# Attention scores as columns of the dense product, and a closed layer's bias and Relu on ScalarE

## The reference, cut to what matters

```python
def _gat_layer(x, src, dst, W, a_src, a_dst, b):
    h = (x @ W).reshape(N, H, C)
    alpha_s = jnp.einsum('nhc,hc->nh', h, a_src)
    alpha_d = jnp.einsum('nhc,hc->nh', h, a_dst)
    e = jax.nn.leaky_relu(alpha_s[src] + alpha_d[dst], NEG_SLOPE)
    m = jax.ops.segment_max(e, dst, num_segments=N)
    ex = jnp.exp(e - m[dst])
    den = jax.ops.segment_sum(ex, dst, num_segments=N)
    alpha = ex / (den[dst] + 1e-16)
    msg = h[src] * alpha[:, :, None]
    return jax.ops.segment_sum(msg, dst, num_segments=N).reshape(N, H * C) + b
for l in range(3):
    x = relu(_gat_layer(x, src, dst, W[l], att_src[l], att_dst[l], bias[l]))
```

## Time and profile before

| | us |
|---|---|
| median of three runs (12354.32 to 12355.26) | 12354.43 |
| the profiled execution's own time | 12329.05 |
| its span, first to last instruction | 12327.0 |
| POOL busy (64% of the span) | 7913.0 |
| PE busy (49%) | 6088.9 |
| DVE busy (41%) | 5089.2 |
| ACT busy (33%) | 4118.9 |

### The profile page before, as it was taken

One profiled execution on the slowest core, in us unless ns is written; L12 is line 12 of the kernel. 1 busy time (PEld: TensorE's weight loads), 2 busy tenths in 40 slices (PEclk: granted clock), 3 DMA queues, 4 the chain that ended last, 5 costly groups with the idle time before them and its releaser, 6 DMA issues.

```text
span 12327.0 us, 135596 instructions
## 1 busy us (share of the span) xinstructions
PE 6088.9 (49%) x36060; PEld 5310.7 (43%) x36060; DVE 5089.2 (41%) x15885; ACT 4118.9 (33%) x10791; POOL 7913.0 (64%) x8254
## 2 busy tenths in 40 slices
PE   0389721445555567997444434434344443444443
PEld 0288611334444446876333333433333343333333
DVE  8555300032222224223444444544444454444445
ACT  0299300034444441101333333333333323333332
POOL 2877777567777750001777777577777757777775
PEclk8555765766666667998555555555555555555555
DMA  9144521222222224886222222222222222222222
GB/s 284 37 103 103 143 59 39 55 53 53 53 53 53 53 49 134 249 255 182 67 67 67 69 67 67 59 64 69 67 68 68 67 54 69 69 67 67 69 67 59
DMA packets 1052978, 1046.24 MB, mean 85 GB/s; under 512 B 641674, under 2 KB 758198, under 8 KB 1051984
## 3 DMA queue, kind: packets, MB, share of 16 engines
q1 hardware_dynamic: 704688, 614.67, 17.2%
q0 software_dynamic: 263776, 336.86, 13.4%
q10 hardware_dynamic: 83808, 86.39, 2.1%
HBM read 938.74 MB, written 100.17 MB: 84 GB/s over the span
## 4 chain that ended last, share of the span: by engine, by line
POOL 61%; issue 21%; PE 11%; DVE 5%; DMA 1%; ACT 1%; DVEq 0%; POOLq 0%; SPq 0%; ACTq 0%; PEldq 0%
POOL sb_HG L586 48%; POOL edge_counts L639 13%; PE sums L1038 4%; PE sums L951 1%; PE psA L1038 1%; PE psB L1038 1%; PE psD L1038 1%; PE psC L1038 1%; DVE sb_HG L1322 1%; DVE sb_ACC L2050 1%; DVE sb_HG L1323 0%; PE psD L935 0%; DMA edge_counts<-sb_HG 0%; PE psB L927 0%; DMA sb_HG<-attention_table,sb_NOW 0%
## 5 line engine op out<-in xcount | busy, mean ns | idle before, releaser
L586 POOL DMA_INDIRECT sb_HG<-attention_table,sb_NOW x4980 | 4727.4, 949 | 2993.5 <-issue 1513.3
L951 PE MATMUL sums<-sb_HG 128*128 128x100 f32 x9984 | 2064.3, 398 | 443.7 <-ACT sb_HG L711 426.9
L951 PEld LDWEIGHTS sums<-sb_HG 128*128 128x128 f32 x9984 | 2031.4, 312 | 453.7 <-ACT sb_HG L711 435.9
L639 POOL DMA_INDIRECT edge_counts<-sb_HG x1625 | 1634.0, 1006 | 697.7 <-issue 490.0
L707 ACT ACTIVATE sb_H<-sb_iota_row,sb_H 128x128 f32<-128x128 f32 x6656 | 2029.2, 388 | 138.1 <-PE sums L951 65.6
L586 POOL DMA_INDIRECT sb_HG<-feature_table,sb_NOW x1612 | 1523.0, 945 | 643.2 <-issue 491.0
L2050 DVE TENSOR_TENSOR sb_ACC<-sb_ACC,sums 128x100 f32 x4992 | 1274.7, 255 | 1155.9 <-PE sums L951 618.9
L961 PEld LDWEIGHTS sums<-sb_HG 128*128 128x128 f32 x6656 | 1313.4, 297 | 328.7 <-issue 328.5
L961 PE MATMUL sums<-sb_HG 128*128 x6656 | 1329.3, 382 | 157.3 <-ACT sb_HG L711 74.5
L800 ACT ACTIVATE psC<-sb_SB 128x128 f32<-128x128 f32 x156 | 43.8, 281 | 3925.8 <-DVE sb_SB L2003 3925.8
L1570 DVE TENSOR_TENSOR sb_ACC<-sb_ACC,sums 128x97 f32 (+1 forms) x3328 | 848.2, 255 | 606.9 <-PE sums L961 127.7
(11 more groups left out here) (507 smaller groups left out, 8917.9 us busy)
## 6 DMA issues: line engine op xcount, KB each, us to landing
sb_HG<-edge_counts SPq DMA_DIRECT2D x1152, 256.0 KB, 3.3
sb_H<-rel_rows SPq DMA_DIRECT2D x312, 512.0 KB, 3.9
sb_HG<-attention_table,sb_NOW POOLq DMA_INDIRECT x4980
sb_HG<-in_edge_attr_dram SPq DMA_DIRECT2D x201, 384.0 KB
edge_counts<-sb_LW ACTq DMA_DIRECT2D x12, 6272.0 KB, 43.1
edge_counts<-sb_HG POOLq DMA_INDIRECT x1625
sb_HG<-feature_table,sb_NOW POOLq DMA_INDIRECT x1612, 2.5
sb_EA<-in_edge_attr_dram SPq DMA_DIRECT2D x201, 128.0 KB, 2.5
```

The source lines that it names most:

```text
L586: pool.indirect_dma_start(to, None, rows, bass.IndirectOffsetOnAxis(ap=index, axis=0)).then_inc(landed, 16)
L639: pool.indirect_dma_start(every_count, bass.IndirectOffsetOnAxis(ap=slot_of[:, f:f + 1], axis=0), tally[:, f:f + 1], None).then_inc(scatte ...
L951: last = nc.tensor.matmul(bank[:, k // 4, k % 4 * width:(k % 4 + 1) * width], HOT[:, hot, k, :], G[:, slot, k, 0:width], start=True, stop= ...
```

## The change

The weights of the three layers move to a tile WG with 104 columns a layer. Columns 96 to 103 are filled once in the setup: for each layer and for source and target, the weights' rows are multiplied with the attention vector and summed by head. The products of a `gat` stage write 104 columns a block, and DVE takes a bank by two copies: 100 columns to ACC and 4 to DD. For layers 1 and 2, the closing of the layer ahead no longer runs over all blocks: DVE multiplies by the inverse denominators group by group as `prepare` of the dense stage (`divide`, three groups ahead), PE transposes ACC, and ACT's copy out of psA becomes a Relu with the bias, which on turned rows is one number for each partition. The last layer is closed as before. SP loads two more bias columns (one small DMA), and DVE waits for the weights ahead of the six multiplications.

```diff
+                sp.dma_start(BCOL[:, 3:3 + LAYERS - 1], L3_bias[0:LAYERS - 1, :].rearrange("l d -> d l")).then_inc(const_in, 16)
-            sp.dma_start(WTS[:, W_GAT:W_GAT + LAYERS, :], L3_W.rearrange("l a b -> a l b")).then_inc(weights_in, 16)
+            sp.dma_start(WG[:, :, 0:D], L3_W.rearrange("l a b -> a l b")).then_inc(weights_in, 16)
...
-                    nc.scalar.activation(zT[0:D, half, :], psA[0:D, :], ACT.Copy).then_inc(SEM["lifted"], 1)
+                    nc.scalar.activation(zT[0:D, half, :], psA[0:D, :], ACT.Copy if bias is None else ACT.Relu, **how)\
+                      .then_inc(SEM["lifted"], 1)
...
-                lift(Stage(f"gat{l}"))
+                lift(Stage(f"gat{l}"), bias=2 + l if l else None)
...
-                        last = nc.tensor.matmul((psD, psC)[half][:, q * D:(q + 1) * D],
-                                                zT[0:D, half, q * P:(q + 1) * P], WTS[:, w, :], start=True, stop=True)
+                        last = nc.tensor.matmul((psD, psC)[half][:, q * width:(q + 1) * width],
+                                                zT[0:D, half, q * P:(q + 1) * P], weights, start=True, stop=True)
...
-                dense_stage(Stage(f"gat{l}"), H, W_GAT + l)
+                dense_stage(Stage(f"gat{l}"), ACC if l else H, WG[:, l, :], WT + HEADS)
...
+            dve.wait_ge(weights_in, (8 + P // DE) * 16)
+            for l in range(LAYERS):
+                for n, r in enumerate((R_ASRC, R_ADST)):
+                    link(v.tensor_tensor(SB[0:D, 0:D], WG[:, l, 0:D], ROWS[0:D, r + l, :], ALU.mult))
+                    link(v.tensor_reduce(WG[:, l, D + n * HEADS:D + (n + 1) * HEADS],
+                                         SB[0:D, 0:D].rearrange("p (h c) -> p h c", h=HEADS), AX.X, ALU.add))
             normalise()
...
-                    part = ds(Q * g, Q)
-                    by_head = [H[:, part, :], HOT_flat[:, 0:Q * D].rearrange("p (b d) -> p b d", b=Q)]
-
-                    dve.wait_ge(SEM["taken"], g + score.base["taken"])
-                    v.tensor_copy(ACC[:, part, 0:D], p)
-                    for n, r in enumerate((R_ASRC, R_ADST)):
-                        last = v.tensor_tensor(by_head[n], p, row(r + l).broadcast_to([P, Q, D]), ALU.mult)
-                    last.then_inc(SEM["scored"], 1)
-                    dve.wait_ge(SEM["scored"], g + (score.base["scored"] + 1))
-                    for n, to in enumerate((ACC[:, part, D:WT], DD[:, part, :])):
-                        last = v.tensor_reduce(to, by_head[n].rearrange("p b (h c) -> p b h c", h=HEADS), AX.X, ALU.add)
-                    return last
-                take(score, attend_to)
+                    part = slice(Q * g, Q * g + Q)
+                    v.tensor_copy(ACC[:, part, :], p[:, :, 0:WT])
+                    return v.tensor_copy(DD[:, part, :], p[:, :, WT:WT + HEADS])
+
+                def divide(g):
+
+                    part = ACC[:, Q * g:Q * g + Q, 0:D].rearrange("p b (h c) -> p b h c", h=HEADS)
+                    by = ACC[:, Q * g:Q * g + Q, D:WT].unsqueeze(3).broadcast_to([P, Q, HEADS, C])
+                    return v.tensor_tensor(part, part, by, ALU.mult)
+
+                take(score, attend_to, prepare=divide if l else None, width=WT + HEADS)
...
-                for h in range(HEADS):
-                    part = ACC[:, :, h * C:(h + 1) * C]
-                    link(v.tensor_tensor(part, part, ACC[:, :, D + h:D + h + 1].broadcast_to([P, NBP, C]), ALU.mult))
-                link(v.tensor_tensor(ACCF, ACCF, over_blocks(row(R_GATB + l)), ALU.add))
-                if l < LAYERS - 1:
-                    link(v.tensor_scalar(H[:, :, :], ACCF, 0.0, None, ALU.max))
+            for h in range(HEADS):
+                part = ACC[:, :, h * C:(h + 1) * C]
+                link(v.tensor_tensor(part, part, ACC[:, :, D + h:D + h + 1].broadcast_to([P, NBP, C]), ALU.mult))
+            link(v.tensor_tensor(ACCF, ACCF, over_blocks(row(R_GATB + LAYERS - 1)), ALU.add))
```

More of the change, by code:

```diff
@@ L134, in gnn_kernel @@
         ones = sb("ones", [P, P])
-        WTS = sb("WTS", [D, 14, D])
+        WTS = sb("WTS", [D, 11, D])
+        WG = sb("WG", [D, LAYERS, WT + HEADS])
         WE = sb("WE", [P, P // DE, D])
         ROWS = sb("ROWS", [P, 7 + 4 * LAYERS, D])
-        BCOL = sb("BCOL", [D, 3])
+        BCOL = sb("BCOL", [D, 3 + LAYERS - 1])
         DD = sb("DD", [P, NBP, HEADS])
@@ L241, in gnn_kernel @@
         W_L0A, W_L0B, W_L0C, W_L0D, W_L11, W_L12, W_IN, W_GCN, W_OUT = 0, 1, 2, 3, 4, 5, 6, 7, 10
-        W_GAT = 11
         TURNED = [W_IN, W_GCN, W_GCN + 1, W_GCN + 2, W_OUT]
@@ L281, in gnn_kernel @@
                  "virtual_made",
-                 "prepared", "flipped", "lifted", "hid_product", "hid_ready", "made", "taken", "scored", "hop_step", "part_step", "parts_made"]
+                 "prepared", "flipped", "lifted", "hid_product", "hid_ready", "made", "taken", "hop_step", "part_step", "parts_made"]
         NAMES += [f"strip_in{n}" for n in range(RING)]
@@ L322, in gnn_kernel @@
             "dense": dense,
-            "scores": dense | {"scored": NG},
             "split": dense | {"part_step": PARTED * NG},
@@ L335, in gnn_kernel @@
         for l in range(LAYERS):
-            PLAN += [(f"gat{l}", "scores"), (f"attend{l}", "attend")]
+            PLAN += [(f"gat{l}", "dense"), (f"attend{l}", "attend")]
         STORED = [16] + [16 + 16 * NG * (n + 1) for n in range(LAYERS)]
@@ L675, in root, with lift @@
                 nc.scalar.activation(to, of, ACT.Sqrt).then_inc(root_ready, 1)
-            def lift(t):
+            def lift(t, bias=None):
+                how = {} if bias is None else {"bias": BCOL[:, bias:bias + 1]}
                 def copy(g, half):
@@ L729, in _ @@
             act.dma_start(cols_now, src_cols).then_inc(cols_in, 16)
-            act.wait_ge(const_in, 14 * 16)
+            act.wait_ge(const_in, 15 * 16)
             lift_mlp(Stage("L0mlp"), 2, 0)
@@ L903, in flip_blocks, with dense_stage @@
                 last.then_inc(SEM["flipped"], 1)
-            def dense_stage(t, z, w):
+            def dense_stage(t, z, weights, width=D):
                 def product(g, half):
@@ L1133, in _ @@
                                  start=True, stop=True).then_inc(feature_totals, 1)
-            dense_stage(Stage("in"), H, W_IN)
-            dense_stage(Stage("gcn"), H, W_GCN)
+            dense_stage(Stage("in"), H, WTS[:, W_IN, :])
+            dense_stage(Stage("gcn"), H, WTS[:, W_GCN, :])
             pe.wait_ge(SEM["taken"], Stage("gcn").end["taken"])
@@ L1554, in _ @@
             dve.wait_ge(x_in, 32)
-            dve.wait_ge(const_in, 14 * 16)
+            dve.wait_ge(const_in, 15 * 16)
+            dve.wait_ge(weights_in, (8 + P // DE) * 16)
[4 more added lines that the diff above has]
+                                         SB[0:D, 0:D].rearrange("p (h c) -> p h c", h=HEADS), AX.X, ALU.add))
             normalise()
@@ L1573, in add_up, with take @@
                     dve.wait_ge(SEM["acc_step"], U * g + (t.base["acc_step"] + k + 1))
-            def take(t, use, banks=(psD, psC), prepare=None):
+            def take(t, use, banks=(psD, psC), prepare=None, width=D):
                 def use_group(g, half):
                     dve.wait_ge(SEM["made"], g + (t.base["made"] + 1))
-                    use(g, banks[half][:, 0:Q * D].rearrange("p (b d) -> p b d", b=Q)).then_inc(SEM["taken"], 1)
+                    use(g, banks[half][:, 0:Q * width].rearrange("p (b d) -> p b d", b=Q)).then_inc(SEM["taken"], 1)
                 def prepare_group(g):
```

## The result

| | before | after |
|---|---|---|
| median of four executions, us | 12354.85 (12354.32 to 12358.67) | 12281.69 (12235.22 to 12284.18) |
| profiled execution, own time | 12329.05 | 12235.22 |
| its span | 12327.0 | 12233.4 |

The change makes the kernel faster: ratio 0.9931, 95% interval 0.9908 to 0.9955. The medians differ by 73.2 us where 67.4 were forecast (12287.0). After's four executions were 12235.22, 12280.0, 12283.38 and 12284.18; the profiled one is the first, and it pulls the ratio down.

The account below looks back on a forecast made before the run. POOL's gathers stay; between them DVE bounds the closes and dense stages. 13.5 + 27.4 + 27.5 - 1.0 = 67.4 us saved: profile 12261.7, median 12287.0 us with the 25.4 us shift; forecast 12279 to 12299, 8 in 10 12272 to 12308.

Parts of the forecast that it names:

- The closes: Between layers, two closes of 14.38 us go, each replaced by one division and a semaphore, 0.62 us: 27.5 us saved.
- their cover: The other twelve divisions hide in DVE's pauses of gat1 and gat2; without them 5.6 us a stage come back.
- The dense stages: gat0, gat1, gat2: DVE's five instructions a group become two, DVE no longer the bound; 13.5 us plus 27.4 us saved.
- columns at 0: Eight further product columns in the dense stages cost nothing, as weight loads set the pace; otherwise some 1 us a stage.
- `in`'s course: Dense stages follow stage `in`: clock rises 12.85 us behind the first transpose and stays high; 25.45 us for gat0.
- The setup: Six multiplications added on DVE may hold up POOL's scatter in the setup, 0 to 1.6 us; -1.0 taken.
- The range: Whole kernel, 8 in 10: 12272 to 12308 us, taking in the forecast of 12279 to 12299 and the falling clock.
- a shift that I carry over: The kernel before's timed median lay 25.4 us above its profiled execution; added to profile 12261.7 to give median 12287.0 us.
- stayed low through a stage: Rival: the clock does not rise in the dense stages; 37.6 us saved, 12317 us. Chance 0.11.
- the swinging clock: Rival: in the dense stages the clock rises and falls again after 6.8 us; 52.6 us saved, 12302 us. Chance 0.12.
- The stores kept up: Rival: SP's table stores, one after another at 2.7 us, become the dense stages' bound; 12323 us. Chance 0.03.
- The attention blocks did not get longer: Rival, slower: DVE's two-input work stretches more of POOL's gathers in the three attention stages; 129 us, 12416 us. Chance 0.03.

Follow-up runs that it names:

- e15: The kernel before, unchanged, run against itself: 12309.83 us, ratio 0.999 (0.997 to 1.001).
- e5: The kernel after with the setup's six multiplications and six sums done ten times over, executed once; no time given, last scatter ended at 2368.37 us.
- e2: The kernel after, unchanged, profiled and timed again: 12249.93 us against 12320.46, ratio 0.9947 (0.9933 to 0.996) to the kernel before.
- e12: The kernel after, unchanged, in a later call: 12282.04 us against before's 12352.44, ratio 0.9936 (0.9923 to 0.995).
- e6: The kernel after with three (gat1, gat2) or four (gat0) further VectorE copies of 384 columns a group: 12294.89 us.
- e4: The closes of after with the kernel before's five VectorE instructions for the scores: 12293.8 us, ratio 0.9979 (0.997 to 0.9988) to the kernel before.
- e1: The kernel before, unchanged, profiled a second time: 12318.69 us, ratio 0.9999 (0.9989 to 1.0008).
- e8: The kernel after with transposes of neighbouring groups in two PSUM banks in turn, executed once; no time given, dense stages 20.10, 24.04 and 21.66 us.
- e9: The kernel after with 24 unread transposes of the identity on TensorE ahead of gat1 and gat2: 12278.11 us, beside 12282.04 of the kernel after.
- e13: The kernel after with 60 unread transposes of the identity on TensorE ahead of gat1 and gat2, executed once: 12227.81 us.

## Why the prediction was off

**The closes**: right, 27.5 us to the tenth, and their cover too: behind the first division the groups keep the 1.48 us of psA's round trip.

**The dense stages**: the mechanism was right (VectorE no longer the bound; 2.52, then 1.39 and 1.48 us a group; columns at 0), the term was too small: 40.9 us for 45.6 in the profile, 44.5 and 47.5 in the two repeats. The step that failed is the moment at which the clock rises: "In `in` it rose 12.85 us behind the first transpose ... Without that wait I expect `in`'s course". That was one execution's number, and it gave gat0 12.85 us and gat1 and gat2 the middle between 12.85 and 8.0. In e15, the kernel before too, the clock rose in `in` between 4.4 and 6.3 us behind the first transpose (PE's transposes of `in`):

```profile
4694.80 1.09 PE L902 MATMUL psA<-sb_ident,sb_H 128*96 128x128 f32 x4 [46.55 <-DVE sb_plan L1587]
...
4699.17 1.06 PE L902 MATMUL psA<-sb_ident,sb_H 128*96 128x128 f32 x4
4701.06 0.60 PE L902 MATMUL psA<-sb_ident,sb_H 128*96 128x128 f32 x4
```

In the nine dense stages of after and its two repeats the pace changed in the third to fifth cycle, in `in` of the earlier trace rows in the sixth, and a stage took 22.2 to 25.2 us, where I had 25.45 and 25.25. With the measured rises of after's profile, 7.9, 5.7 and 10.0 us, the prediction's own sum gives 23.2, 23.3 and 25.1 us for the measured 23.15, 23.13 and 24.98: nothing else in the term was off. The forecast lay at the late end of a spread, not outside it: in e5, whose dense stages are those of after, the clock rose 10.4, 13.2 and 10.1 us in, the stages took 24.28, 26.25 and 25.06 us, and the term would have been 41.3.

**The setup**: -1.0 should have been 0. With these two corrections, 45.6 + 27.5 = 73.1 us, beside 73.2, 70.5 and 70.4 in the three comparisons. 12287.0 was 5.3 us above the measured median, and that is 4.7 and 1.0, less 0.4 by which before's median moved.

**The range** failed for a second reason. It was made from the unknowns of the change, 12279 to 12299 for the forecast and 12272 to 12308 with the rivals, on "a shift that I carry over" of 25.4 us between profile and median. This shift was not a property of the kernel but the place of one execution in a spread of 20 to 50 us; for the kernel after it was 46.5 us in the first comparison, and -1.8 (e2) and -0.2 (e12) in the repeats. The table of before showed only three runs within 0.9 us, but the profiled execution beside them, 25 us off, was the sign. After's profiled execution fell 45 to 49 us below the other three, which lie at 12280.0 to 12284.2, inside the range, and it moved the ratio's time to 12269.6. Either correction would have kept that in, as can be said now: with half of the 25.4 us added on either side, the range would have begun near 12259; with the 5.7 us of the two terms, at 12266.3.

**The rivals**: the clock rose and stayed up in every dense stage of the kernel after; it fell again with VectorE slowed (e6), and stayed low through a stage with VectorE's six instructions (e4) and, in one stage of e1, with the five of before. For the swinging clock of the Trainium skill's page (TensorE: Matmul & The Clock Gate, section "A second HAM failure mode: psum-queue depth-cycling") the dense stages of the kernel after gave no case, nor did those of e8 with two banks for the transposes. The stores kept up at 1.4 us a group; the last landed in 2.67 us. The attention blocks did not get longer with the change: 2081.3, 2081.0 and 2082.0 before, 2080.8, 2081.9 and 2080.7 after.

## What to carry to other kernels

Take a loop's new pace from another stage of the same trace that already lacks the engine you are freeing; that gave 2.52, 1.39 and 1.48 to 0.01 us. But the moment at which the clock rises is not a constant of a stage: in `in` it was 5.6, 10.6 and 12.8 us in three executions of the same kernel. It goes into a sum as a range, taken from several executions, and a profiled execution that stands apart from its timed runs means a spread that belongs into the range too. Once the engine that makes the others wait is found, look at the clock at the start of a stage: filling the pause ahead of it was worth 2 to 4 us a stage here.

## What the hardware showed that I had not expected

In e9 TensorE's clock was at its high level (1.00) at the end of the two attention layers ahead of gat1 and gat2, though it had paused 1.65 us between its last batches; in e2 it had fallen to 0.50 before the last batch ended. After a pause of 5.32 us (e9) the dense stage began at 0.50, after one of 1.39 us (e13) at 1.00.

VectorE's instructions of 384 columns are shown with 0.55 us and start 0.46 us apart. Adding their durations overstates a loop: six took 2.91 us, not 3.3.

A scatter of POOL that started inside a two-input VectorE instruction ended 0.84 us behind that instruction's end, whether it was 0.25 or 7.09 us long (some others in before's setup 1.18 us behind); alone it takes 0.96. VectorE was held in turn, 0.29 to 0.33 for 0.25 us, when both started within 0.05 us.
